# Query normalisation moved from VectorE to GpSimd in a four-layer cross-attention network on one core

## What is computed

```
q = layernorm(q_x, ln_q_g, ln_q_b) @ Wq.T                     # layer 1, attention 2
h = layer_norm(x, ln1_g, ln1_b); x = x + mha(h, h, h, ...)    # layer 2, attention 3
h = layer_norm(x, ln2_g, ln2_b); x = x + mha(h, enc, enc, ...)# layer 2, attention 4
h = layer_norm(x, ln3_g, ln3_b); x = x + relu(h @ w1 + b1) @ w2 + b2
layernorm(x) = (x - mean) * rsqrt(var + 1e-5) * gamma + beta
```

## Time and profile before

| | us |
|---|---|
| median of 3 runs | 1057.02 (1055.11 to 1057.31) |
| profiled execution | 1057.35 |
| its span, first to last instruction | 1055.4 |
| PE busy | 997.7 (95%) |
| DVE busy | 793.3 (75%) |
| ACT busy | 635.5 (60%) |
| POOL busy | 320.3 (30%) |

### The profile page before, as it was taken

One profiled execution on the slowest core, in us unless ns is written; L12 is line 12 of the kernel. 1 busy time (PEld: TensorE's weight loads), 2 busy tenths in 40 slices (PEclk: granted clock), 3 DMA queues, 4 the chain that ended last, 5 costly groups with the idle time before them and its releaser, 6 DMA issues.

```text
span 1055.4 us, 38728 instructions
## 1 busy us (share of the span) xinstructions
PE 997.7 (95%) x16957; PEld 721.3 (68%) x16957; DVE 793.3 (75%) x2232; ACT 635.5 (60%) x938; POOL 320.3 (30%) x389
## 2 busy tenths in 40 slices
PE   8879998999999999999999999899999999999996
PEld 5657765576776676777777677566777677777674
DVE  4697899867477655778877889998567774568986
ACT  5346665666776555565645666566777766464652
POOL 4021235611000103455550323553010010236542
PEclk9999999999999999999999999999999999999999
DMA  7000000000000000000001000000000000000001
GB/s 263 3 23 23 3 3 3 2 2 2 3 3 3 2 13 21 11 2 2 2 1 33 2 13 3 3 2 2 3 2 3 2 4 2 1 2 2 2 1 41
DMA packets 13720, 13.59 MB, mean 13 GB/s; under 512 B 617, under 2 KB 13170, under 8 KB 13298
## 3 DMA queue, kind: packets, MB, share of 16 engines
q1 hardware_dynamic: 13554, 11.11, 3.4%
HBM read 9.02 MB, written 2.10 MB: 11 GB/s over the span
## 4 chain that ended last, share of the span: by engine, by line
PE 37%; DVE 9%; ACT 5%; POOL 2%; issue 2%; POOLq 0%; ACTq 0%; DVEq 0%
PE pair L711 7%; PE pair L919 6%; PE pair L914 4%; PE pair L698 4%; PE pair L785 3%; PE pair L818 2%; PE pair L938 2%; DVE mx L1373 2%; ACT PT L1014 2%; PE pair L686 2%; ACT KQ L980 2%; PE pair L952 2%; PE pair L705 1%; PE pair L795 1%; PE pair L967 1%
## 5 line engine op out<-in xcount | busy, mean ns | idle before, releaser
L1014 ACT ACTIVATE PT<-pair 128x1024 f32<-128x1024 f32 x184 | 180.4, 1030 | 118.8 <-PE pair L919 109.4
L1373 DVE TENSOR_REDUCE mx<-pair 128x16 f32<-128x1024 f32 x184 | 218.6, 1216 | 43.1 <-PE pair L919 42.6
L919 PEld LDWEIGHTS pair<-KQ 32*128 32x128 f32 (+3 forms) x4416 | 170.5, 157 | 36.3 <-issue 3.0
L919 PE MATMUL pair<-KQ 32*128 32x128 f32 (+3 forms) x4416 | 180.1, 253 | 1.7 <-ACT PT L1014 0.6
L711 PE MATMUL pair<-xf,W_all 128*128 128x512 f32 x336 | 177.5, 624 | 2.1 <-ACT xf L980 1.2
L1400 POOL TENSOR_SCALAR ve<-mv 128x4 f32<-128x4 f32 x64 | 16.8, 263 | 486.5 <-DVE mv L1093 472.4
L980 ACT ACTIVATE KQ<-pair,c 128x512 f32<-128x512 f32 x160 | 100.5, 692 | 42.4 <-PE pair L711 41.8
L686 PE MATMUL pair<-warm 128*128 128x512 bf16 (+3 forms) x581 | 111.7, 387 | 12.8 <-DVE Y L1177 4.3
L938 PE MATMUL pair<-PT,V 128*32 128x64 f32 x5120 | 94.0, 221 | 2.2 <-ACT PT L1014 0.7
L980 ACT ACTIVATE V<-pair 64x512 f32<-64x512 f32 x128 | 79.2, 619 | 24.3 <-PE pair L818 22.6
L938 PEld LDWEIGHTS pair<-PT,V 128*32 128x32 f32 x5120 | 78.3, 110 | 22.1 <-issue 9.0
(11 more groups left out here) (121 smaller groups left out, 1802.6 us busy)
## 6 DMA issues: line engine op xcount, KB each, us to landing
W_all<-weights SPq DMA_DIRECT2D x1, 2880.0 KB, 13.2
Xin<-x SPq DMA_DIRECT2D x8, 256.0 KB, 3.6
C<-ctx SPq DMA_DIRECT2D x8, 256.0 KB, 4.7
out<-X SPq DMA_DIRECT2D x8, 256.0 KB, 2.3
row<-rows SPq DMA_DIRECT2D x1, 1024.0 KB, 6.1
c<-const SPq DMA_DIRECT2D x1, 504.0 KB, 5.7
W_all<-weights SPq DMA_DIRECT2D x1, 192.0 KB, 2.9
c<-const SPq DMA_DIRECT2D x1, 87.0 KB, 2.1
```

Of the source, the lines that this page charges most:

```text
L919: last[u] = pe.matmul(banked[u // 2][:, at:at + 2 * S], stationary[rows_, seq].rearrange("p r t -> p (r t)"), moving[rows_, seq].rearrange ...
L1014: act.activation(PT[:, place, :], banks.of("B", a, s, v)[:], ACT.Exp, scale=float((D // (2 * PAIRS[a])) ** -0.5)).then_inc(*banks.drain((" ...
L1373: dve.tensor_reduce(dst, banks.of("A", a, s, v)[:].rearrange("p (u m t) -> p u m t", u=2, t=S), AX.X, ALU.max).then_inc(*banks.drain(("A", ...
```

## The change

POOL normalises the rows for the queries, right behind the reciprocals of their deviations, in the same step of its list. It gets a function `normal`, which waits for POOL's own `rstd` and does DVE's four instructions. DVE's list loses its 32 `nq`; all other names keep their order. Who waited for DVE's "q" waits for POOL's: PE's step `q`, and POOL's own `wo` and `down`. The lists of PE, ACT and POOL are as they were.

```diff
--- before.py
+++ after.py
@@ "DVE" @@
-        0.2.2 sum; 0.2.0 nq; 0.2.1 z; 0.2.2 nkv n1; 0.2.0 mx0 mx1; 0.2.3 O0; 0.2.1 n3; 0.2.0 mx2 mx3; 0.2.3 O1; 0.2.0
+        0.2.2 sum; 0.2.1 z; 0.2.2 nkv n1; 0.2.0 mx0 mx1; 0.2.3 O0; 0.2.1 n3; 0.2.0 mx2 mx3; 0.2.3 O1; 0.2.0 nm; 0.2.1
...
                     elif name == "q":
-                        pe.wait_ge(*vec.at("q", a, s))
+                        pe.wait_ge(*pool.at("q", a, s))
                         turn(Y[s], use)
...
-                    elif name == "nq":
-                        norm(Y[s], X[s], "q", a, s)
...
+                def normal(dst, src, *tag):
+
+                    i = lane(tag)
+                    g_.wait_ge(*pool.at("rstd", *tag))
+                    for j in range(NT):
+                        g_.tensor_scalar(dst[:, j, :], src[:, j, :], mv[i][:, j, 0:1], rstd[i][:, j:j + 1],
+                                         ALU.subtract, ALU.mult).then_inc(*pool.mark(*tag))
...
                     elif name == "n3q" or (name == "addwo" and a > 3) or (name == "addff" and a == 3):
                         deviation(False, "q", a, s)
+                        normal(Y[s], X[s], "q", a, s)
                     elif name == "wo" and a == 3:
-                        g_.wait_ge(*vec.at("q", 2, s))
+                        g_.wait_ge(*pool.at("q", 2, s))
                         add_bias(name, a, s)
                     elif name == "down":
-                        g_.wait_ge(*(banks.ready("x", 3, s) if a == 3 else vec.at("q", a, s)))
+                        g_.wait_ge(*(banks.ready("x", 3, s) if a == 3 else pool.at("q", a, s)))
```

More of the change, by code:

```diff
@@ L257 @@
[L257 to L261, removed]
@@ new lines @@
+        0.4.0 mx0 mx1; 0.4.2 addwo; 0.4.0 mx2; 0.4.0 mx3; 0.4.3 O0; 0.4.0 nm; 0.4.1 mx0 mx1; 0.4.3 O1; 0.4.0 mrow;
+        0.4.1 mx2 mx3 nm mrow; 0.4.3 addwo; 0.5.0 O0; 0.5.0 O1 addwo; 0.5.1 O0 O1; 0.4.2 mx0 mx1 mx2; 0.5.1 addwo;
+        0.4.2 mx3 nm mrow; 0.4.3 mx0; 0.5.0 addff qm; 0.4.3 mx1 mx2 mx3; 0.5.0 km; 0.4.3 nm; 0.5.0 lrow; 0.4.3 mrow;
+        0.5.2 O0 O1; 0.5.0 mx0 nm mrow; 0.5.2 addwo; 0.5.3 O0 O1; 0.5.1 addff qm; 0.6.0 O0 O1 sum; 0.5.1 km; 0.6.0 n1;
+        0.5.1 lrow; 0.5.3 addwo; 0.5.1 mx0 nm; 0.5.1 mrow; 0.6.0 leaky; 0.5.2 addff qm km; 0.6.1 O0 O1; 0.6.0 qm;
@@ L296 @@
[L296 to L300, removed]
@@ L306 @@
[L306 removed]
+        n3q; 1.2.2 O1; 1.1.3 mrow; 1.2.2 kvstats sum nkv n1; 1.2.1 z; 1.2.0 mx0 mx1; 1.2.1 n3; 1.2.0 mx2 mx3; 1.2.3
+        O0; 1.2.0 nm; 1.2.1 n3q; 1.2.0 mrow; 1.2.3 O1; 1.2.2 z; 1.2.3 kvstats; 1.2.2 n3; 1.2.3 sum; 1.3.0 O0 O1; 1.2.2
+        n3q; 1.2.3 nkv n1; 1.2.1 mx0 mx1; 1.3.0 addwo; 1.2.1 mx2 mx3 nm mrow; 1.2.2 mx0 mx1; 1.2.3 z n3; 1.3.0 silu0
+        silu1 silu2; 1.2.2 mx2; 1.3.0 silu3; 1.2.3 n3q; 1.2.2 mx3; 1.3.1 O0; 1.2.2 nm; 1.3.1 O1; 1.3.0 addff; 1.2.2
@@ new lines @@
+        mx0 mx1; 1.4.3 O0; 1.4.1 mx2 mx3; 1.4.0 mx0; 1.4.2 addwo; 1.4.0 mx1; 1.4.3 O1; 1.4.0 mx2 mx3 nm mrow; 1.4.3
+        addwo; 1.4.1 nm mrow; 1.5.0 O0 O1 addwo; 1.5.1 O0 O1; 1.4.3 mx0 mx1; 1.4.2 mx0 mx1; 1.5.1 addwo; 1.4.2 mx2
+        mx3; 1.4.2 nm; 1.5.0 addff; 1.4.3 mx2; 1.4.2 mrow; 1.4.3 mx3 nm; 1.5.0 qm km; 1.4.3 mrow; 1.5.0 lrow; 1.5.2 O0
+        O1; 1.5.0 mx0 nm; 1.5.2 addwo; 1.5.0 mrow; 1.5.3 O0 O1; 1.5.1 addff qm km lrow; 1.5.3 addwo; 1.6.0 O0; 1.5.1
+        mx0; 1.5.1 nm mrow; 1.6.0 O1; 1.5.2 addff; 1.6.0 sum n1; 1.5.2 qm; 1.6.1 O0 O1 sum n1; 1.5.2 km; 1.5.3 addff
@@ new lines @@
+        nm; 1.7.2 sum; 1.6.3 mrow; 1.7.1 leaky; 1.7.0 lrow; 1.7.2 n1; 1.7.1 qm; 1.7.0 mx0; 1.7.3 O0 O1 sum; 1.7.0 nm;
+        1.7.1 km; 1.7.3 n1; 1.7.0 mrow; 1.7.1 lrow; 1.7.2 leaky qm; 1.7.1 mx0 nm; 1.8.0 O0; 1.7.3 leaky; 1.8.0 O1;
+        1.7.1 mrow; 1.7.2 km; 1.8.0 sum; 1.7.2 lrow; 1.7.3 qm; 1.8.0 n1; 1.7.3 km; 1.8.1 O0 O1; 1.7.2 mx0 nm; 1.7.3
+        lrow; 1.7.2 mrow; 1.8.1 sum; 1.7.3 mx0 nm; 1.8.1 n1; 1.8.2 O0 O1; 1.7.3 mrow; 1.8.2 sum n1; 1.8.3 O0 O1 sum;
+        1.8.0 leaky; 1.8.3 n1; 1.8.2 leaky; 1.8.1 leaky; 1.8.3 leaky
```

47 lines of the change are left out of this document (18 added, 29 removed).

## The result

The changed kernel takes 1112.36 us, the median of 4 runs (1110.37 to 1114.98), against 1056.51 for the kernel before in the same session: a ratio of 1.0529, interval 1.0503 to 1.0555. It is slower by 5.3%. The forecast was no change, 1057.7 us, and its range ended at 1066.0.

A forecast was written before the change was run, and what follows sets the result against it. PE, busy 95%, was taken as the bound. DVE's relief of -1.15 us plus 1.80 us of shortfalls gave +0.65 us on the median of 1057.02, so 1057.7 us, no change; range 1054.5 to 1066.0.

The forecast's parts named there:

- I take 0.40 us, next to the midway value, because one input is read and one written.: POOL's normalisation of 128x128: assumed 0.40 us an op, bounds 0.33 to 0.48, making a four-op step 1.48 us.
- the 0.60 that I called not excluded: POOL's op: up to 0.60 us if a software loop handles columns dearly; about +14 us, left outside the range.
- shortfalls: Distances from reciprocals' end to PE's transposes: twelve of 32 are below the new 1.62 us path, lacking 2.21 us together.
- the 1.16 absorbed: PE's 1.16 us wait for DVE at 210.58: swallows attention 2, stream 2's shortfall of 0.41, leaving 1.80 us lost.
- POOL's op is dearer: Rival at twelve to twenty queries with little slack: slower, +5.1 us at 0.48 us an op; chance 0.26.
- What queues behind it on POOL: POOL's next items come up to 1.56 us later; x1 of stream 3 has 1.79 us slack; cost nothing.
- DVE's relief, -1.15 us: Three PE waits that DVE ends behind removed steps, 0.38, 0.31 and 0.46 us, all taken as gained.
- Rival C: PE's idle time: DVE's relief reaches PE through ACT, ending a quarter of 21.8 us, -3.7 us net; chance 0.16.
- DVE and POOL block each other: Rival at attention 2's and 3's queries: DVE's z and silu collide with POOL's normalisation, +3.45 us; chance 0.12.

The follow-up runs named there:

- two sets of forms: Kernel before with eleven, then nine, forms of POOL op added three times each where POOL idles, results unused; 1056.31 and 1056.17 us, a single run each.
- six-query version: Kernel before with only six of the 32 queries, those of 3.36 us or more distance, normalised on POOL; 1066.98 us, ratio 1.0085.
- shared version: Kernel before with each query's four pieces shared, DVE normalising three and POOL the last; 1055.14 us, ratio 0.9991.
- product-only kernel: Changed kernel with one 128x512 product with the reciprocals replacing the four pieces, mean not subtracted; 1057.3 us, ratio 1.0013.
- the constants: Changed kernel with constants 0.0 and 1.0 in place of the mean and reciprocal columns, queries not normalised; 1086.5 us, ratio 1.0281.
- four-query version: Six-query version without attention 2 stream 0 and attention 4 stream 0 of the second group, leaving four queries on POOL; 1057.71 us, ratio 1.0009.
- late signal: Kernel before, DVE still normalising, with two idle powers on POOL ahead of the queries' reciprocals; 1117.68 us, ratio 1.0566.

## Why the prediction was wrong

- **What bounds the kernel.** Right: PE bounds it, and "any new wait of PE is lost time in full unless a later wait swallows it" held for the 35.8 us of new waits, which all came back in the time, and more. DVE's relief of 30.1 us was off the path.
- **"I take 0.40 us, next to the midway value, because one input is read and one written."** This step failed. The op takes 0.813 us in the kernel. Both my bounds were below it, and so was the 0.60 that I called not excluded. The upper bound of the slope, 2.05 ns an element, came from a two-input add, on the belief that an op with one input cannot be slower than one with two. The runs show 3.31 ns for it against 1.65. The fixed part, "0.23 us" from an op on constants, is 0.38 with two columns. That makes 0.38 + 124 x 3.31 ns = 0.79 us, near the 0.80 measured alone. At the measured step of 3.15 us and path of 3.30 the prediction's own shortfalls are 37.0 us; less the 1.16 absorbed and the 1.15 taken as gained that is +34.7, or 1091.7 us. So the price of the op accounts for most of the miss, and the 20.7 us left to 1112.4 are what the sum had at nothing: the clock, POOL's queue, and a rest.
- **The page's rule.** The prediction gave beside this the rule of the Trainium skill, GPSIMD Engine Reference, § 4.1 Engine selection, that one-input elementwise work is roughly line-rate there and two-input work about 2x slower than on VectorE. The runs do not agree for this op: 813 ns against 343 on DVE for the same four-piece step's instruction.
- **The path and its shortfalls.** Right in form at five lengths, to 1.2 us. The rival "POOL's op is dearer" named the mechanism and the point from which it decides (a path of 1.74: +7.1 us measured, 2.1 worked out), and the chance of 0.26 rested on a range of the op that was too low. Its price at 0.60 us, +14, left the range; the truth lay behind that.
- **The clock, missing from the sum.** I priced a wait by its length. Eleven half-clock stretches made PE's busy time 15.8 us longer, and fillers in the waits gave 13.1 us back. The kernel before showed it in small: behind the wait at 159.29 its transposes kept full clock, but a stretch at half clock begins at 162.38. Whether it comes behind waits this short differs from one execution to the next, as the two sets of forms show.
- **"What queues behind it on POOL ... Cost nothing."** Right at my op, wrong at the real one, and I looked in one place only: x1 of stream 3. What costs is that the keys' reciprocals and stream 1's stand behind a step nobody is in a hurry for. It is part of the loss; the six-query version puts its two places at 3.6 and 3.8 us, half clock behind them included.
- **DVE's relief, -1.15 us.** This step failed too, at a small price. "Three remain ... all taken as gained": with the old path all three waits stand at 0.38, 0.31 and 0.46 us. DVE having no idle time between a removed step and the wait was not enough for the relief to reach it. Rival C fell as well.
- **DVE and POOL block each other.** The ops named there, L1277 and L1313, take 508 and 732 ns in the changed kernel and took 535 and 732 before, so this rival has next to no part in the result (the keys' pieces, L1098, went from 336 to 367 ns, 1 us in all). The mechanism is real: DVE's pieces go from 343 to 386 ns beside POOL's in the shared version, and at 183 us eight DVE ops take 2.16 or 5.04 us. The Trainium skill, SBUF — State Buffer, § Who interferes with whom, describes an exclusive lock, one engine stopped while the other works; the two outcomes at 183 us, each with one side held up, agree with it.

What was to be seen in the profile: DVE's busy time fell to 763.2 (forecast about 757), its waits for PE grew by more than the 51.7 us, and the first line, the op's 0.33 to 0.48 us, already said that the forecast had fallen.

## What to carry to other kernels

Where an operation moves to an engine on which the trace has never seen it, a bound from another kind of operation is no bound: measure that form alone, in a stretch in which the engine idles, before a sum is made on it. On POOL the normalisation is cheaper as two two-input ops than as TENSOR_SCALAR with two scalars. Before a step goes into another engine's queue, list for every place what stands behind it and who wants that first, as a step with 8.7 us to spare can hold up one with 1.5. And a wait of the bounding TensorE costs more than its length where the clock falls behind it, which fillers in the wait can give back; here that was so with 35.8 us of new waits, and did not show with 3.5 or 12.2.

## What the runs showed of the hardware

- POOL (fp32, 128 partitions, alone): TENSOR_SCALAR 0.53 us at 128 elements and 1.49 at 512 with one step of arithmetic on a constant, 0.65 and 1.92 with two steps, 0.80 and 2.07 with two columns as scalars. TENSOR_TENSOR 0.20 us at 4 elements and 1.04 at 512, 1.06 with one input a column spread along the row. I had expected the one-input op to be the faster.
- In the changed kernel TensorE's granted clock fell to 1.2 GHz within or behind nine waits of 0.6 to 4.2 us, seven of them for POOL's Y, for 44.4 us in all with two more stretches (10.2 us before), and PE's busy time grew by 15.8 us with no instruction more.
- Two ops that meet on DVE and POOL end in one of two ways, by small shifts in time: eight DVE ops 2.16 us and POOL's product 1.87, or 5.04 and 1.08. Behind the second PE waited 2.4 to 3.3 us at that place and not at all behind the first, where a wait of 0.8 to 1.1 us for nm came instead in five of seven traces. One program shows both, at the same time within 0.1%.
- The length of such a half-clock stretch differs from run to run at the same place. In the product-only kernel the one around 540 us lasted 13.66 us, where the kernel before has 3.41:

```profile
539.39:553.05 13.66, 12.93 (x108) 10.39 (x112) 7.83 (x23) 4.75 (x9) 5.55 (x8) 0.50 0.00 1
```

PE fell back by 4.3 us between the sixteenth and the seventeenth query there, with no wait to show for it. The traces of the constants, the four-query version, the shared version and the late signal have 13.65 us at the same place of the program too. It is a likely reason that runs of the product-only kernel spread over 1052.7 to 1063.5 us (granted clock 0.998 in the fastest, 0.988 in the slowest), and that the profiled executions of the last three are 2.9 to 5.9 us above their medians; what makes it long stays open.
